# Single products for the maxima, 64 channels of gate and up in one product, and earlier loads of the experts, in a gated cross-attention and mixture-of-experts kernel

## What is computed

```python
q, k, v = layernorm(x) @ w_q.T, ctx @ w_k.T, ctx @ w_v.T         # 32, 8 and 8 heads of 16
attn = softmax(where(pad or not causal, -inf, q @ k.T / 4))
x = x + tanh(g_xattn) * ((attn @ v) @ w_o.T + b_o)
xt = layernorm(x)
scores = softmax(xt @ Wg.T); topi = best 4 of the best 2 groups
y = sum over the 4 experts of scores * ((silu(xt @ W1.T) * (xt @ W3.T)) @ W2.T)
z = (silu(xt @ Ws1.T) * (xt @ Ws3.T)) @ Ws2.T
x = x + tanh(g_ffn) * (y + z)
```

## Time and profile before

| what | us |
|---|---|
| median of 3 runs (lowest, highest) | 1355.91 (1350.62, 1359.08) |
| the profiled execution, its span | 1353.09, 1351.3 |
| stretch 0 to 107 (projections), TensorE busy | 100.58 |
| stretch 140 to 400 (attention), TensorE / VectorE busy | 239.6 / 231.9 |
| stretch 440 to 532 (closing), TensorE busy | 85.76 |
| stretch 532 to 765 (shared), TensorE busy | 228.15 |
| stretch 765 to 1351 (experts), TensorE busy | 556.20 |
| TensorE over the span | 1272.3 (94%), granted clock 0.979 |

### The profile page before, as it was taken

One profiled execution on the slowest core, in us unless ns is written; L12 is line 12 of the kernel. 1 busy time (PEld: TensorE's weight loads), 2 busy tenths in 40 slices (PEclk: granted clock), 3 DMA queues, 4 the chain that ended last, 5 costly groups with the idle time before them and its releaser, 6 DMA issues. The chain is left out here.

```text
span 1351.3 us, 27369 instructions
## 1 busy us (share of the span) xinstructions
PE 1272.3 (94%) x8553; PEld 936.9 (69%) x8554; DVE 646.7 (48%) x1861; ACT 586.4 (43%) x1016; POOL 642.8 (48%) x722
## 2 busy tenths in 40 slices
PE   8998999999997998999999799999999999999995
PEld 5554544444443357778767589999989988889894
DVE  4345788888896654686304113232343333333300
ACT  1222566666663223222222145555545444445452
POOL 6000333333332431443455266666666666666664
PEclk8999999999998997999999899999999999999998
DMA  9452333333343404000013225555555554665433
GB/s 338 150 162 89 111 109 100 97 107 99 95 126 120 159 1 187 32 32 32 32 55 103 96 52 139 141 142 142 137 132 141 142 139 129 157 174 129 91 71 39
DMA packets 73615, 152.94 MB, mean 113 GB/s; under 512 B 10725, under 2 KB 16357, under 8 KB 72793
## 3 DMA queue, kind: packets, MB, share of 16 engines
q1 hardware_dynamic: 52104, 100.27, 22.1%
q0 software_dynamic: 21456, 51.97, 18.4%
HBM read 97.56 MB, written 52.23 MB: 111 GB/s over the span
## 5 line engine op out<-in xcount | busy, mean ns | idle before, releaser
L202 DVE CUSTOM_DVE_ANT_0 a_mb<-a_mb,late 128x128 f32<-128x128 f32 (+3 forms) x512 | 244.4, 510 | 50.8 <-PE a_mb L183 44.1
L1439 DVE CAST e_w<-e_w 128x480 fp32r<-128x480 f32 x135 | 75.5, 568 | 360.4 <-DMA e_w<-in_w2T 360.4
L634 ACT ACTIVATE a_at<-a_eb 128x1024 f32<-128x1024 f32 (+3 forms) x256 | 179.6, 705 | 102.4 <-PE a_eb L696 101.8
L570 POOL TENSOR_SCALAR_AFFINE_SELECT a_at<-a_at 128x256 f32<-128x256 f32 x256 | 105.5, 412 | 225.4 <-ACT a_at L634 225.2
L1593 PE MATMUL e_yps<-e_w,e_hT 128*128 x711 | 197.3, 404 | 0.9 <-ACT e_hT L1504 0.9
L1572 PE MATMUL e_gate<-e_w,e_xT 128*128 x948 | 169.8, 328 | 8.5 <-DVE e_w L1448 7.8
L1572 PEld LDWEIGHTS e_gate<-e_w,e_xT 128*128 128x128 f32 x948 | 156.7, 190 | 20.7 <-issue 16.4
L1572 PE MATMUL e_up<-e_w,e_xT 128*128 x948 | 170.6, 329 | 0.0
L1572 PEld LDWEIGHTS e_up<-e_w,e_xT 128*128 128x128 f32 x948 | 149.8, 188 | 0.0
L1593 PEld LDWEIGHTS e_yps<-e_w,e_hT 128*128 128x128 f32 x711 | 128.1, 189 | 25.5 <-issue 1.2
L1470 POOL TENSOR_TENSOR e_hT<-e_hc,e_hT 128x384 fp32r<-128x384 f32 x79 | 84.3, 1067 | 118.9 <-ACT e_hc L1505 118.9
(11 more groups left out here) (235 smaller groups left out, 1844.5 us busy)
## 6 DMA issues: line engine op xcount, KB each, us to landing
e_w<-in_w13T SPq DMA_DIRECT2D x16, 1408.0 KB
dq<-p_parts SPq DMA_DIRECT2D x32, 256.0 KB, 2.4
a_q<-dq SPq DMA_DIRECT2D x64, 128.0 KB
do<-a_o SPq DMA_DIRECT2D x32, 256.0 KB, 2.1
e_w<-in_w2T SPq DMA_DIRECT2D x16, 512.0 KB
a_k<-dk SPq DMA_DIRECT2D x64, 98.0 KB
e_w<-in_ctxT SPq DMA_DIRECT2D x4, 1024.0 KB, 13.9
e_w<-in_x SPq DMA_DIRECT2D x4, 1024.0 KB, 13.2
```

Of the source, the lines that this page charges most:

```text
L202: eng.tensor_tensor_reduce(out=b[:, 0:w], in0=b[:, 0:w], in1=io["late"][:, SEQ - w:SEQ], scale=1.0, scalar=3 * NEG, op0=ALU.add, op1=ALU.m ...
L570: eng.affine_select(out=square, in_=square, compare_op=ALU.is_ge, fill=0.0, base=0, pattern=[[0, 2], [1, P]], channel_multiplier=-1).then_ ...
L634: eng.activation(at[r % 2][:, ch, 2 * hp:2 * hp + 2, ch * P:SEQ], eb[hp][:, :, ch * P:SEQ], ACT.Exp, scale=0.25).then_inc(s_exp, 1)
```

## The change

Four edits, each with the others in one file.

1. *Maxima products singly.* `max_pair` becomes `find_maxima`, one product m of 16 (`OPS`, in the order of the old pairs), with a wait of its own for its own bank. A step now is: product 2u + 1, the exponent products in the order that alternates the halves of the array, product 2u + 2, value products; the first product of a round stands at the end of the round before (`first_maxima`). Twice a round (before products 4 and 12) the ring skips a bank, by `SLOTS`. The transpose of the maxima goes into the unused corner of the exponents' bank (`turned`) instead of a ring bank, at ch = 1 instead of ch = 0, and its copy goes from VectorE to ScalarE (`take_row`), ahead of the exponentials of that step.
2. *The last 64 channels.* The weights are laid out anew: gate has 704 + 64 columns, of which the last 64 are up's last channels, and up has 640. The sixth unit is 12 products of 128 columns of weights; its up half is copied from rows 64 to 127 of the gate bank. A gate product now waits for both ScalarE's silu and its copy of two units before. The load of the next batch's x waits for gate instead of up.
3. *The experts' loads.* `load_expert` is cut in two. The 1408 KB of gate and up go when the up products of the last tile of expert e - 2 are done, the rest when its down products are. Expert 1's load is moved past the barrier, to the beginning of `stage_experts`, with its wait for the stores.
4. *The last result.* The last group of 128 tokens of the shared part is scaled and added by VectorE in one instruction instead of by ScalarE and GpSimd, and SP stores it after that.

```diff
+OPS = [(t, j, ch) for pair in PAIRS for j in range(2) for t, ch in pair]
+NOPS = len(OPS)
+SLOTS = [m + (m >= NOPS // 4) + (m >= 3 * NOPS // 4) for m in range(NOPS)]
+PERIOD = NOPS + 2
...
+WHOLE, LEFT = (NS - 1) * P, SHARED - (NS - 1) * P
+WIDE = (SHARED + LEFT, WHOLE)
...
-def max_pair(eng, io, i, r, turn, j):
-
-    u = i * CH * HG + turn * HG + 2 * j
-    if place(turn, j, 1) - RING == SKIPPED:
-        eng.wait_ge(io["s_rmax"], u + 1)
-    elif not isinstance(i, int) or u:
-        eng.wait_ge(io["s_rmax"], u)
-    for at, (t, ch) in enumerate(PAIRS[turn]):
...
+def free(m):
+
+    slot = SLOTS[m] - RING
+    while slot % PERIOD not in SLOTS:
+        slot -= RING
+    return SLOTS.index(slot % PERIOD) + slot // PERIOD * NOPS + 1
+
+
+def find_maxima(eng, io, i, r, m):
+
+    t, j, ch = OPS[m]
+    if not isinstance(i, int) or i * NOPS + free(m) > 0:
+        eng.wait_ge(io["s_rmax"], i * NOPS + free(m) + 1)
...
+            def take_row(i, r, t):
+                if after(i, 1):
+                    eng.wait_ge(s_row[(r - 1) % NB], ROWS * (t + (r - 1) // NB + 1))
+                eng.wait_ge(io["s_mt"], i + 3)
+                eng.activation(io["mrow"][(r + 1) % 2], turned, ACT.Copy).then_inc(s_mr, 1)
...
                 for ch in range(CH):
                     for j in range(2):
+                        m = 2 * (2 * ch + j) + 1
                         if exists(i + AHEAD):
-                            max_pair(eng, io, i + AHEAD, (r + AHEAD) % NB, ch, j)
-                        exp_unit(i, r, ch, j)
+                            find_maxima(eng, io, i + AHEAD, (r + AHEAD) % NB, m)
+                        exp_unit(i, r, ch, j, (1 - OPS[m][0], OPS[m][0]))
+                        if m + 1 < NOPS and exists(i + AHEAD):
+                            find_maxima(eng, io, i + AHEAD, (r + AHEAD) % NB, m + 1)
+                        elif m + 1 == NOPS and exists(i + AHEAD + 1):
+                            first_maxima(i + AHEAD + 1, (r + AHEAD + 1) % NB, t + (r + AHEAD + 1) // NB)
                         pv_units(i, r, 2 * ch + j)
-                    if ch == 0 and exists(i + 1):
-                        turn_maxima(eng, io, r + 1, (i + AHEAD) * CH * HG + HG if exists(i + AHEAD) else NIT * CH * HG + 1)
...
                 if i >= 2:
                     eng.wait_ge(s_act, i)
+                    eng.wait_ge(s_upc, i)
                 multiply(i, n, 0, gate, s_gate)
-                if i >= 2:
-                    eng.wait_ge(s_upc, i)
-                multiply(i, n, 1, up, s_up)
+                if n < NS - 1:
+                    multiply(i, n, 1, up, s_up)
...
-            eng.wait_ge(s_down, NT + 1)
-            eng.wait_ge(io["s_base"], 16 * NT)
-            load_expert(eng, io, 1, 1)
...
         @block.sync
         def _(eng):
+            eng.wait_ge(io["s_base"], 16 * NT)
+            load_first(eng, io, 1, 1)
+            load_second(eng, io, 1, 1)
             with eng.Fori(1, E // 2) as u:
                 for r in range(2):
                     free = eng.value_load(io["first"][0:1, bass.ds(u * 2 + r - 1, 1)], min_val=0, max_val=TILES)
                     eng.wait_ge(s_w, (u * 2 + r) * LOAD)
+                    eng.wait_ge(s_up, free)
+                    load_first(eng, io, u * 2 + r, r)
                     eng.wait_ge(s_down, free)
-                    load_expert(eng, io, u * 2 + r, r)
+                    load_second(eng, io, u * 2 + r, r)
```

More of the change, by code:

```diff
@@ L1215, in _ @@
                                   w[p, 0, cols].bitcast(F32), ALU.subtract).then_inc(s_low, 1)
+            eng.wait_ge(s_down, NT + 1)
+            last = x1[BATCH - 1][:, CH - 1, :]
+            eng.scalar_tensor_tensor(out=last, in0=yps[(NT - 1) % 2][:], scalar=tg[:, 0:1], in1=last,
+                                     op0=ALU.mult, op1=ALU.add).then_inc(s_v, 1)
+            compared.append(next(done))
         @block.scalar
```

144 lines of the change are left out of this document (75 added, 69 removed).

## The result

The changed kernel takes 1497.26 us (median of 4 runs, 1482.97 to 1504.89), the kernel before beside it 1354.45 (4 runs): ratio 1.1041, 95% interval 1.095 to 1.1131. It is 10% slower, where 1.9% faster was forecast. The profiled execution took 1497.03 us, with a span of 1495.3 and a mean granted clock of 0.858 (before: 0.979).

A forecast was written before the change was run, and what follows sets the result against it. In attention the loop of pair wait, product and VectorE was taken as the limit, in later stages TensorE with few waits. Gains of 6.6 + 5.6 + 4 + 9.2 = 25.4 us gave 1330 us, 8-in-10 range 1317 to 1345.

The forecast's parts named there:

- Attention, -6.6 forecast: Attention: single maxima products shorten a round from 9.22 to 9.0 us, over 30 rounds 6.6 us less.
- the 8.8 of the bounds: Attention: a gap-free handover would give rounds of 8.8 us, 12 us less.
- The slow rival: Attention: a lone product loses the overlap, 0.22 instead of 0.11 us; 27 us more in attention, 1364 in all; chance 0.04.
- the sum by it was 8.85: Attention: by the row-group rule, steps with 512-wide exponents would be some 0.1 us shorter and the round 8.85.
- Experts, -9.2 forecast: Experts: sooner loads start VectorE's splitting some 4.5 to 5.5 us sooner; 9.2 us less, lower bound 5.
- all seven gate waits: Experts: gate products wait for VectorE's splitting seven times, the longest 1.5 us; all were to go.
- GpSimd's 4.73: Start of experts: GpSimd's first product of tile 0 took 4.73 us beside VectorE's splitting; it could limit the gain to 1.2.
- Shared part, -5.6 forecast: Shared feed-forward: one 2.76 us unit fewer in 4 batches saves 11.0, new waits cost 4.3 and 1.1; 5.6 us less.
- the new wait for the low part: Shared feed-forward: down products wait 1.52 us for GpSimd's low part in batches 0, 2 and 3; 4.3 us in all.
- the one for the routing tables: Shared feed-forward, batch 1: TensorE reaches the last two routing tables before VectorE finishes; about 1.1 us waited.
- Going over to the experts, -4 forecast: From shared part to experts: TensorE starts 4.3 us sooner, GpSimd may be shut out; 4 us less, bounds 1.2 and 5.9.
- the free start of the experts: Rival: attention gains fully (8.85 a round, 11 us) and the experts' new start runs free, 1.6 more; 1324 us, chance 0.2.

The follow-up runs named there:

- VectorE light: VectorE's maxima over every second column only: 1358.56 us on the changed kernel, 1337.54 us on the kernel before.
- The narrower products: Kernel before with every maxima product 256 columns wide: 1365.73 and 1398.29 us in two runs.
- the old attention: Kernel before with every part of the change but the attention's: 1372.35 us, ratio 1.0104.
- the version with late first loads: Kernel before with all but the attention's part, first half of later experts' loads behind the same wait as the second: 1342.7 us, ratio 0.9913.
- the joint pairs: Changed kernel with both maxima products ahead of the exponents and both their waits ahead of the first: 1506.9 us; with the turn of the maxima first too, 1492.34 us.

## Why the prediction was wrong

**Attention, -6.6 forecast, +132 measured (with the round behind it).** The step that failed is "Followed through one round, alternately taking the later of 'bank free' and 'TensorE there', I get 8.85 to 9.0". It treated a lone wait as a handover between two engines. But TensorE works in order, and the prediction had said it itself: behind each added wait stand the exponent or value products. It then priced that by ScalarE's idle time, not by TensorE's own. The rows above price it: 0.79 for 0.27 in such steps, two or three times a round, against steps elsewhere that are mostly 0.05 and once 0.25 shorter. Rounds came out at 9.3 to 10.0 where 9.0 was forecast. Even with VectorE light the changed order took 8.98, so the 9.0 forecast for the full VectorE, and the 8.8 of the bounds all the more, were out of reach. The pair had its merit: its wait came once, ahead of work that was done anyway.

**The clock was in no term and in no rival.** The earlier trace rows say 1.00 at 91.74 busy, and I took that as given. Up to 0.8 us more a round (9.2 to 10.0) were followed by half the clock, at which a round is 5.5 longer than before (9.2 to 14.7). That is nearly all of the loss: 22 rounds ran so. The slow rival (1364, from lone products at 0.22 instead of 0.11) had the right sign by the wrong mechanism; with VectorE made light the changed order costs 0.26 a round, not 0.9. The rule on row groups that the prediction took from the Trainium skill, "TensorE: Matmul & The Clock Gate", Part 3, does not show here: the sum by it was 8.85, and exchanging the exponents, which puts one of the same group first, left the rounds at 9.29 to 9.62 and the starts inside a step as they were. The same page, the Trainium skill, "TensorE: Matmul & The Clock Gate", Part 1, says that the default state is throttled and activity releases it. The narrower products and the light VectorE agree in kind (less streamed in 9.06 us fell; rounds of 8.98 held), though the narrower products also held in rounds of 9.05 once the clock was back. That part describes the fall as following an idle stretch, and in a second case frequent short idles between groups of products. Here the longest wait that TensorE's totals show between 142 and 196 us of the changed kernel was 0.3 us, and the clock fell all the same and stayed down.

**Experts, -9.2 forecast, +20.1 measured.** The first part was right: the splitting starts sooner and all seven gate waits go. What failed is what the sooner splitting was priced at: nothing, with a lower bound of "5, if the low half disturbs gathers and scatters". The prediction had the right row in hand, GpSimd's 4.73 beside VectorE's splitting, and used it for tile 0 alone; the same collision, moved onto `e_hT`, came seven times, at 2.6 us each, and behind five of them the clock was down. The 20.1 are made up so: TensorE idles 10.4 us more over the stage, and the clock takes 9.9 more. On the page quoted there, the Trainium skill, "SBUF — State Buffer", section "Who interferes with whom": VectorE in a two-port mode and GpSimd exclude each other for a whole instruction. The runs show 5.50 us beside nine instructions; here the row, not the rule of one instruction, gave the size.

**Shared part, -5.6 forecast, -3.3 measured (-3.9 with the old attention).** The mechanism was right, term by term: the new wait for the low part, 4.3 forecast, is 4.1 in three waits; the one for the routing tables, 1.1 forecast, is 1.7. With 11.0 gone that would leave 5.2 less; where the last 1.3 to 1.9 went stays open (TensorE idles 5.7 more over the part, which is these two terms).

**Going over to the experts, -4 forecast, -4.5 measured.** TensorE idles 2.65 instead of 7.15, and "about 3" was named. GpSimd's first products beside the splitting are still long: in the version with late first loads one `e_hT` takes 4.45 and costs TensorE 1.4, inside the experts' 569.0.

Forecast for the parts without attention and experts: 9.6 less; measured 7.8 to 8.4, in which the closing stage's 2.7 more are not counted. A slip in the rivals changes nothing: for the free start of the experts the sum takes 1.6, by its own bound it would be 5.9 - 4 = 1.9.

**What stays open.** Whether waits as such or the smaller share of streaming lowers the clock, and what picks the moment: the same rounds fell at 205, 186 and 185 us in three kernels with the same attention or nearly so. Why the changed order costs 0.26 a round with a light VectorE. Why rounds in the changed kernel grow from 9.29 to 9.97 before the clock goes. Whether the ring's new places or ScalarE's row copy make the rounds of 9.5 of the joint pairs: no run had them alone. And why the changed order never gets the clock back: its half-clock rounds are 14.72, those of the narrower products, which got it back, 12.26, and those of the kernel before with a pause, which never did, 13.93; no run changes only that.

## What to carry to other kernels

A wait put in the middle of an in-order engine's queue is paid by everything behind it: price it on that engine first. Where TensorE is near the point at which its granted clock falls, as in a stage with many narrow products bound by another engine, add one pause a round to the kernel you have and look at the clock; if half a microsecond a round costs a hundred over the stage, every change there has to be judged by the clock before anything else. And a transfer that is made sooner moves the work that it feeds: look up what that work will stand beside, before counting the wait it saves.

## What the runs showed of the hardware that was not expected

- One added wait a round in the kernel before, in rounds of 9.2, turned 1354 us into 1487: the granted clock went to 0.50 at about 150 us and stayed, at 97% busy. The first such wait was 0.77 us, and the clock fell within 2 us of it. TensorE's busy share at full clock tells nothing of it: 99% in the changed kernel and 87% in the one with narrower products, which both fell, 92% before, which did not.
- The clock can come back inside the stage: 0.50 from 201 to about 255 us, then 1.00 for the rest, in the kernel before with narrower products.
- A series of VectorE's instructions, one behind the other, can hold a GpSimd instruction to its end and not only for one instruction: 5.50 us for 1.01 beside nine of them, and up to 5.80 in the same run; the longest `e_hT` in the kernel before was 1.53.
- After a wait of 2.65 us among the experts the granted clock was down for some 6 us. Of the 14 waits of 2.4 to 2.9 us in two kernels, 12 were followed by a lower clock.
